# Two places a head for the later layers' stages, with square roots, weight roundings and norms on GpSimd, in a one-core decoder layer

## The reference, cut to what matters

```python
x = layernorm(x + attn(x, Wq, Wk, Wv, Wo))          # 32 query heads, 8 key heads of 64, rope, causal
x = layernorm(x + xattn(x, fside, ctx))             # per batch: quantised gate/up product, silu, quantised down product
x = layernorm(x + ffn(x, up, down, scales))         # signs of the weights, relu, 512 -> 2048 -> 512

def quant_linear(x, w):                             # used twice in xattn
    s = max(sqrt(max(colmax|x|, EPS) / max(colmax|w|, EPS)), EPS)
    xs, ws = x / s, w * s
    x_scale, w_scale = rowmax|xs| / 127, rowmax|ws| / 127
    return (round(xs / x_scale) @ round(ws / w_scale).T) * x_scale * w_scale.T

def layernorm(x): return (x - mean(x)) / sqrt(var(x) + 1e-5)
```

## Time and profile before

| | us |
|---|---|
| median of three executions | 1481.77 |
| lowest and highest | 1480.76, 1482.88 |
| profiled execution, its own time | 1484.37 |
| its span, first to last instruction | 1482.6 |
| PE, DVE, ACT, POOL busy | 1313.8, 998.1, 940.2, 751.6 |

### The profile page before, as it was taken

The page is one execution under the profiler, slowest core; times in us unless marked ns, Lnnn a source line. Parts: engine busy times, 40 slices in busy tenths (PEclk is TensorE's granted clock), DMA queues, the critical chain, the costliest instruction groups (busy, mean ns, idle before and its releaser), DMA issues.

```text
span 1482.6 us, 25047 instructions
## 1 busy us (share of the span) xinstructions
PE 1313.8 (89%) x7099; PEld 1081.3 (73%) x7112; DVE 998.1 (67%) x2435; ACT 940.2 (63%) x2197; POOL 751.6 (51%) x641
## 2 busy tenths in 40 slices
PE   3799999999999999898889888878897889899996
PEld 2588888888888877677777777767776667677775
DVE  3467777767777767878776786778777676744222
ACT  2576677676777776676767766666776584644332
POOL 3456555556556665465535464556441263536343
PEclk9799999999999999999999999999999999999999
DMA  4422212222122233222122222221235311010000
GB/s 170 147 75 65 58 50 67 64 78 60 50 61 58 72 89 100 72 64 58 50 62 76 58 51 58 79 57 47 52 86 162 139 37 49 18 40 3 26 29 28
DMA packets 54852, 98.78 MB, mean 67 GB/s; under 512 B 11744, under 2 KB 13792, under 8 KB 53728
## 3 DMA queue, kind: packets, MB, share of 16 engines
q1 hardware_dynamic: 54752, 97.57, 23.3%
HBM read 51.39 MB, written 4.19 MB: 37 GB/s over the span
## 4 chain that ended last, share of the span: by engine, by line
PE 63%; DVE 14%; ACT 10%; issue 7%; POOL 4%; DMA 1%; ACTq 0%; DVEq 0%; POOLq 0%; SPq 0%
PE m L1588 26%; PE ps_s L1588 8%; PE ps_o L1645 6%; PE ps_t L1633 6%; PE m L1873 6%; PE ps_s L1887 3%; PE ps_t L1887 3%; ACT pT_hi L1028 2%; DVE pT_lo L1308 2%; PE m L1655 2%; ACT probs L1020 2%; DVE o_sum L1261 1%; DVE probs L1247 1%; POOL y L963 1%; DVE sm_a L1361 1%
## 5 line engine op out<-in xcount | busy, mean ns | idle before, releaser
L1020 ACT ACTIVATE probs<-probs,neg_max 128x128 f32<-128x128 f32 (+3 forms) x512 | 285.2, 559 | 179.0 <-DVE neg_max L1247 178.4
L1308 DVE TENSOR_TENSOR pT_lo<-ps_t,pT_hi 128x512 fp32r<-128x512 f32 (+1 forms) x384 | 220.7, 595 | 148.0 <-ACT pT_hi L1028 145.8
L1633 PE MATMUL ps_t<-ident,probs 128*128 128x128 f32 x1280 | 188.3, 278 | 91.8 <-DVE pT_lo L1308 76.3
L1588 PE MATMUL ps_s<-k_st,q_st 128*128 128x256 f32 (+2 forms) x1024 | 236.0, 354 | 0.3 <-DVE neg_max L1247 0.3
L1633 PEld LDWEIGHTS ps_t<-ident,probs 128*128 128x128 f32 x1280 | 146.3, 142 | 122.4 <-DVE pT_lo L1308 94.8
L1247 DVE CUSTOM_DVE_ANT_0 probs<-ps_s,mask 128x128 f32<-128x128 f32 (+3 forms) x512 | 228.1, 482 | 6.8 <-PE ps_s L1588 6.6
L881 POOL TENSOR_TENSOR o_lo<-o_sum,o_hi 128x512 fp32r<-128x512 f32 x64 | 82.7, 1293 | 252.1 <-ACT o_hi L1042 252.1
L1028 ACT ACTIVATE pT_hi<-ps_t 128x512 fp32r<-128x512 f32 (+1 forms) x384 | 185.7, 518 | 5.6 <-PE ps_t L1633 2.5
L934 POOL TENSOR_TENSOR hid_lo<-hid,hid_hi 128x512 fp32r<-128x512 f32 x64 | 83.9, 1313 | 166.2 <-ACT hid_hi L1212 166.1
L1645 PE MATMUL ps_o<-pT_hi,v_st 128*128 128x256 f32 (+2 forms) x512 | 167.8, 339 | 0.0
L1588 PEld LDWEIGHTS ps_s<-k_st,q_st 128*128 128x128 f32 x1024 | 154.0, 195 | 4.0 <-DVE neg_max L1247 0.5
(11 more groups left out here) (251 smaller groups left out, 3064.9 us busy)
## 6 DMA issues: line engine op xcount, KB each, us to landing
q_st<-q_tmp SPq DMA_DIRECT2D x512, 64.0 KB, 2.0
raw<-in_wq_t SPq DMA_DIRECT2D x32, 256.0 KB, 3.0
k_st<-k_st SPq DMA_DIRECT2D x64, 128.0 KB, 2.4
raw<-in_wo_t SPq DMA_DIRECT2D x32, 256.0 KB, 3.0
raw_b<-in_ffn_t SPq DMA_DIRECT2D x10, 512.0 KB, 7.5
y<-in_x_t SPq DMA_DIRECT2D x4, 1024.0 KB, 10.8
raw<-in_wkv_t SPq DMA_DIRECT2D x16, 256.0 KB, 3.7
y<-in_x SPq DMA_DIRECT2D x4, 1024.0 KB, 5.7
```

Of the source, the lines that this page charges most:

```text
L1020: act.activation(probs[:, h % 2, SO[i]:SO[i] + SW[i]], probs[:, h % 2, SO[i]:SO[i] + SW[i]], ACT.Exp, bias=neg_max[:, h % 2, i:i + 1], sca ...
L1308: dve.tensor_tensor(pT_lo[:, d, :], ps_t[:, (h + k) % 2, 0:P * w].rearrange("p (w c) -> p w c", c=P), f32(pT_hi[:, d, :]), ALU.subtract).t ...
L1588: i = pe.matmul(dst, a, c, start=(j == 0), stop=(j == len(terms) - 1))
L1633: i = pe.transpose(ps_t[:, (h + k) % 2, P * c:P * (c + 1)], probs[:, h % 2, at:at + P], ident[:, :])
```

## The change: two places a head, smaller stages, and work moved to GpSimd

- **Places.** Every engine but SP has two places for stages. DVE: `dve` after the first low part and the sum of the old head, `dve2` right after the reciprocal. ACT: `act` after `high_p(2)`, `act2` at the end. PE: `pe` before the third group of transposes, `pe2` right before `values`. POOL's places are at the start of b, after `repeat_r(0)` (ticks with h = 2) and after `rotate_k` (h = 3); SP's at the start of b and before `move_k`.
- **Stages.** Norms, roundings and `add` go one tile a stage; `scales` is a stage of its own (`xscale`, `wscale`). A new hand-placed schedule for ticks 0 to 72; that of the ticks from 64 on is shifted.
- **Work.** All 20 square roots become a `pow` with exponent 0.5 or -0.5 on POOL (128x4 elements; the norms' reciprocals on DVE go). The centring products of N and B move from DVE to POOL, those of F stay. The roundings of all weights, and those of `xs` for batches 0 and 1, move from ACT to POOL.
- **Timing of the batches.** The last third of batch 1's chain A (its row and its four products, silu and `a`) falls into ticks 66 to 72. Batch 1's chain B starts at tick 73, not 67, and its `x2T` at 92, not 88. Batch 2's `wmax` and the load for it come after tick 64. Four of six signs in steps 8 to 15 move past tick 64.

```diff
-A_SLOW = """
-    0 dve colmax0 colmax1
-    1 dve colmax2 colmax3
...
-    7 dve xabs0 xabs1
-    8 act xround0
-    9 act xround1
...
+A_0 = """
...
+    6 dve2 colmax0
+    7 dve colmax1
+    8 dve colmax2
+    9 dve colmax3
+    9 pe2 colx
+    10 dve ratio
+    11 pool root
+    11 dve2 reps
...
+    14 dve xabs0
+    14 pool ws0 ws1 ws2 ws3
+    15 dve xabs1
+    16 dve xscale
...
+    18 pool xround0 xround1 xround2 xround3
+    18 dve2 xq
...
+N_0 = """
+    1 dve var0
+    2 dve var1
+    2 dve2 var2
+    3 dve var3
+    4 dve rstd
+    6 pool power norm0 norm1 norm2 norm3
...
+A_1 = """
...
+    62 act wqT0
+    62 pe2 wT1
+    65 act wqT1
+    66 pe wrow
+    66 act wrow
+    67 pe prod0
+    67 dve prod0
...
+    70 dve prod3
+    71 act silu
+    72 dve a
...
-    17 dve var20 var21
-    18 act std2
-    19 dve y20 y21
+    17 dve var20 var21 var22 var23 rstd2
+    18 pool power y20 y21 y22 y23
...
-    7 dve var
-    8 act std
-    12 dve norm
-    12 sp out
+    7 dve var
+    7 pool power
+    9 dve norm
+    10 sp out
...
+    (SLOTS, "N", 2, N_FAST),
     (SLOTS + 1, "T", 0, T_STAGES),
-    (SLOTS + 5, "A", 2, A_FAST),
-    (SLOTS + 3, "B", 1, B_FAST),
-    (SLOTS + 24, "B", 1, X2T),
+    (SLOTS + 7, "A", 2, A_FAST),
+    (SLOTS + 9, "B", 1, B_FAST),
+    (SLOTS + 28, "B", 1, X2T),
...
+            def rounded(tile, scale):
+                return pool.tensor_scalar(tile, tile, scale, ROUND, ALU.mult, ALU.add)
+
+            def centered(n, mv, inv, t):
+                return pool.tensor_scalar(y[:, n, :], y[:, n, :], mv[:, t, 0:1], inv[:, 1, t:t + 1], ALU.subtract, ALU.mult)
...
+                if name == "root":
+                    after(pool, "A", "dve", b, "ratio")
+                    ends(pool.tensor_tensor(sm_a[:, 3, :], sm_a[:, 3, :], half_pow[:, 0, :], ALU.pow), "A", "pool")
+                    return
...
                         high_p(n, h, 2)
                         if h == 1 and nxt:
                             high_q(u + 1, (0, 1))
+                        if half == 1:
+                            later("act", slot(g, b, h))
...
                         if half == 1:
-                            later("act", slot(g, b, h))
+                            later("act2", slot(g, b, h))
...
-                if name == "root":
-                    after(act, "A", "dve", b, "ratio")
-                    i = act.activation(sm_a[:, 3, :], sm_a[:, 3, :], ACT.Sqrt)
...
                             if k == 0 and (prev or h > 0):
                                 add_o(n - 1, (h - 1) % G, u * 2 + (h - 1) // 2)
+                            if k == 0 and half == 1:
+                                later("dve", slot(g, b, h))
...
                         dve.reciprocal(r_inv[:, :, h // 2, h % 2], row_sum[:, h % 2, :]).then_inc(r_done, 1)
+                        if half == 1:
+                            later("dve2", slot(g, b, h))
...
-                        if half == 1:
-                            later("dve", slot(g, b, h))
...
+                        if half == 1:
+                            later("pe", slot(g, b, h))
                         transpose_probs(n, h, 2)
                         if more:
                             scores(*ahead, 2)
                             scores(*ahead, 3)
-                        if half == 1:
-                            later("pe", slot(g, b, h))
...
+                        if half == 1:
+                            later("pe2", slot(g, b, h))
                         values(n, h, b % 2)
...
-                        after(pe, "B", "dve", b, "y21")
+                        after(pe, "B", "pool", b, "y23")
```

More of the change, by code:

```diff
@@ new lines @@
+"""
+N_1 = """
+    9 dve2 var0
+    10 dve2 var1
+    11 dve var2
+    12 dve var3
+    19 dve rstd
+    20 pool power
+    22 pool norm0 norm1 norm2
+    23 pool norm3
+"""
+B_0 = """
+    23 sp wT
+    25 dve2 wmax
+    27 sp w
+    30 dve2 colmax
+    31 pe colx
+    31 dve ratio
+    31 pool root
+    31 dve2 reps
+    32 pe rows
+    32 act roww
+    32 dve2 xs
+    33 dve xabs
+    33 dve2 xscale
+    34 dve wabs
+    34 act xround0
+    34 pool ws0 ws1
+    34 dve2 wscale
+    35 act xround1
+    35 pool wround0
+    35 dve2 xq
+    36 pe xT
+    36 dve wq
+    36 act xqT
+    36 pool wround1
+    36 pe2 wT
+    37 act2 wqT
+    38 pe wrow
+    38 act wrow
+    38 pe2 prod0
+    39 dve prod0
+    39 pool add0
+    39 pe2 prod1
+    40 dve prod1
+    40 pe2 prod2
+    42 dve prod2
+    42 pool add1
+    42 pe2 prod3
+    43 pool add2
+    44 dve prod3
+    45 dve var20
+    45 dve2 var21 var22
+    46 dve var23
+    46 pool add3
+    46 dve2 rstd2
+    47 pool power y20
+    48 pool y21 y22
+    50 pool y23
+    58 pe x2T0
+    58 act hi0
+    58 dve2 lo0
+    59 pe x2T1
+    59 act hi1
+    59 dve2 lo1
+    60 pe x2T2
+    60 act hi2
+    60 dve2 lo2
+    61 pe x2T3
+    61 act2 hi3
+    62 dve lo3
@@ L154 @@
+"""
+N_FAST = """
+    0 dve var0 var1
+    1 dve var2 var3 rstd
+    2 pool power norm0 norm1 norm2 norm3
 """
@@ L173 @@
     2 dve ratio
[L174 to L205, removed]
+    2 pool root
+    3 dve reps
+    4 pe rowsw rowsx
+    4 act roww
+    5 dve xs0 xs1
+    5 pool ws0
+    6 pool ws1
+    7 pool ws2
+    8 pool ws3
+    6 dve xabs0 xabs1 xscale
+    7 act xround0 xround1
+    8 act xround2 xround3
+    9 dve wabs0 wabs1 wscale xq
+    10 pool wround0 wround1
+    10 pe xT0 xT1
+    11 act xqT0 xqT1
+    11 pool wround2 wround3
+    13 dve wq
+    14 pe wT0 wT1
+    14 act wqT0 wqT1
+    16 pe wrow
+    16 act wrow
+    17 pe prod0
+    17 dve prod0
+    18 pe prod1
+    18 dve prod1
+    19 pe prod2
+    19 dve prod2
+    20 pe prod3
+    20 dve prod3
+    20 act silu
+    22 dve a
 """
@@ L210 @@
     2 dve ratio
[L211 to L222, removed]
+    2 pool root
+    3 dve reps
+    4 pe rows
+    4 act roww
+    4 pool ws0
+    5 pool ws1
+    5 dve xs xabs xscale
+    6 act xround0 xround1
+    7 dve wabs wscale xq
+    8 pool wround0 wround1
+    8 pe xT
+    8 act xqT
     10 dve wq
@@ L594, in run @@
                 later(eng, tick)
+                later(eng + "2", tick)
         def tile_of(p, j):
@@ L643, in ends, with at_tick @@
             i.then_inc(done[chain + e], 1)
-        def at_tick(eng, tick):
-            return [(chain, b, name) for e, chain, b, name in SCHEDULE.get(tick, []) if e == eng]
+        def at_tick(place, tick):
+            return SCHEDULE.get((tick, place), [])
         block = es.enter_context(nc.Block())
@@ new lines, in a @@
+                ends(i, "A", "pool")
+            def b_(b, name):
+                if name == "root":
+                    after(pool, "B", "dve", b, "ratio")
+                    ends(pool.tensor_tensor(sm_b[:, 3, 0:2], sm_b[:, 3, 0:2], half_pow[:, 0, 0:2], ALU.pow), "B", "pool")
+                    return
+                if name == "power":
+                    after(pool, "B", "dve", b, "rstd2")
+                    ends(pool.tensor_tensor(norm[:, 1, :], norm[:, 0, :], half_pow[:, 1, :], ALU.pow), "B", "pool")
+                    return
```

406 lines of the change are left out of this document (201 added, 205 removed).

## The result

The changed kernel takes 1503.81 us (median of 4 runs, 1497.09 to 1506.81) against 1481.37 (4 runs), a ratio of 1.0144, 95% interval 1.0104 to 1.0183. The forecast, 1449 with a range up to 1478, was wrong in sign and range. The profiled execution took 1497.09, the fastest of the four, with a span of 1495.3; beside the profiled execution of before (1484.37) that is 12.7 us more, where 32.9 less were forecast. So 45.6 us have to be found.

What follows compares the result with a forecast made beforehand. PE was taken as the bound, with only its waits and clock to win. Seven steps -47.3, last step -3, feed-forward periods +4.4, +5 and +8 gave -32.9 us on 1484.37: 1451.5, as a median 1449, range 1424 to 1478.

Steps and rivals of the forecast that it cites:

- the term for POOL's blocks: Feed-forward periods: five norm and y2 blocks on POOL, 6.1 us each, cost +8 us net, from 0 to 20.
- +4.4: Feed-forward periods: PE gets batch 1's products and row, 4.4 us more.
- +5: Feed-forward periods: batch 1's last low part bare at tick 96, about 2 us, and x2T0 late; together 5 us more.
- PE's own work (15.7): Seven steps: PE's work for later layers, 17.2 us less two transpose groups slipping into the last step, 15.7 kept.
- the 444.9: Seven steps: their time without later layers, seven times the 63.56 us of eight heads of attention alone.
- 18 us left of 64: Seven steps: of 43 us of plain waits and 21 us lost to PE's clock, 18 us remain.
- Rival 3: DVE's first place: stalls only move, staying at some 50 us; 1481 us; chance 0.06.
- ticks 11 and 31: Steps: DVE's reps waits for the power behind rotate_k on POOL, 1.2 + 1.0 us, twice, within the 18.
- the stall at 610 us: Kernel before: two centring products hold DVE 3.99 us; PE's third transposes wait 4.08 us, clock down until about 623.
- Last step: Last step: loses batch 1's products, a table load and four signs, gains 24 transposes, three copies and wq: -3 us.
- 1 (dear power): POOL's queue: 17 places pay each us of a power over the first; at 5 us, 1517 us; chance 0.12.
- 2 (blocks take more: POOL's five blocks and dense queue cost 20 us, not 8, second half keeps 22: 1465 us; chance 0.17.

Runs made afterwards that it cites:

- e8: The changed kernel with twelve more GpSimd instructions of 128x512 behind its end, two of each form: subtract with a pointer 1.56 us, multiply and add with two pointers 0.77.
- e1: The changed kernel with the centring products from tick 64 on back on DVE, powers left on POOL: 1474.4 us, ratio 0.9953.
- e2: The changed kernel with all centring products of the later layers back on DVE, powers left on POOL: 1468.1 us, ratio 0.9919.
- e9: The changed kernel with centring still on POOL in its places, but as multiplication by 1/std and addition of -mean/std: 1468.7 us, ratio 0.9919.
- e12: As e9, with batch 1's down-weight maximum and batch 0's last low part at tick 62 moved to DVE's second place: 1467.5 us, ratio 0.9903.
- e3: The changed kernel with each of its 20 powers done twice, first into unused columns: 1516.5 us, ratio 1.0229.
- e15: As e9, with batch 1's last steps, chain B and x2T earlier, e12's edit, and xq ahead of the weights' maxima in the tail: 1456.8 us, ratio 0.9841.
- e4: The changed kernel with batch 3's whole chain A three ticks later: 1505.0 us, ratio 1.0162.
- e6: As e2, with batch 2's chains A and B two ticks later and batch 3's chain N ten ticks later: 1470.4 us, ratio 0.9922.
- e7: As e2, with only the four column maxima of batch 3's chain A two ticks later: 1468.0 us, ratio 0.9911.

## Why the prediction was wrong

**The step that failed is the price of POOL's centring.** The prediction said: "For a rounding or centring of 128x512 the ends are the one-input copy, 0.65, and the two-input subtraction, 1.28. I take 1.28, as both do arithmetic per element." For the rounding that held from above (0.70 to 0.79). The centring takes 2.07 to 2.14 (e8: the subtraction alone 1.56), and one row for two operations with different arithmetic was not a bound. The five blocks of the tail take 9.3 and not 6.1 us, 16 us more of POOL's time, but e1 puts the cost at 29 us and e2 and e9 the whole of it at 35: a late block is paid again by what stands behind it and by PE's clock (0.86 in the first period). In the sum it sits in the term for POOL's blocks, +8, from 0 to 20. With all other terms of the tail as forecast (334.3 us) that term came out at 32.5, far above its upper end, and the range of the whole was too narrow with it.

**How much that explains.** By the medians the forecast is 54.8 us too low (1503.8 against 1449), and 35 to 36 of them go with the centring on POOL or its dear form (e2, e9). The kernel without them, at 1468, is inside the range but still 19 us over the forecast: that rest is mostly the steps, below.

**The tail, once that is taken out, is near the forecast, in part by luck:** 341.2 us in e2 against 342.3. But the forecast had 25.6 us of centring on POOL in it, and e2 has none there; e9, whose blocks stay on POOL and take 4.5 us where I had 6.1, has 346.7. So something else in the tail costs more than I gave it, and the single terms (+4.4, +5) were not measured. The two places that I named are there, `x2T0` late behind the y2 block (8.73 us) and the last low part bare at tick 96 (5.16, I had about 2 for it). What I did not see is the longest: the norm block of batch 3 ahead of `ws3`. I counted what waits for `hid_lo` behind the block and not what else stands behind it in the same queue.

**The steps: 478.6 forecast, 498.6 measured, 492.0 without the centring on POOL.** This is the second term that failed. With PE's own work (15.7) and the 444.9 taken as they were, the "18 us left of 64", a judgement, should have been 31 (492.0 - 444.9 - 15.7), with the centring on POOL 38; PEclk came to 0.98, not the 0.99 that I asked for. The part that I named went: the wait for the low part is 14.9 us, under the 25 that I set. In its place came the wait of the reciprocals' transposes, 23.1 from 5.4. Rival 3 ("The first place lies between two low parts, so it delays the very instruction PE waits for") was right in its mechanism for part of the time: in e12 two stages moved from the first place to the second cut the last step by 3.3 us or more. In ticks 11 and 31 I gave DVE's wait for the power 2.2 us each; it was 1.44 and 0.54. I missed tick 48, where the power stands behind two centred tiles: 4.73.

**What the prediction misread in the rows.** It blames the stall at 610 us on the size of the stage: "two centring products keep DVE for 3.99 us in one place". In the trace of before these are one product of 3.54 us and one of 0.53, and the long one ends 0.3 us after a row of four two-input instructions on POOL. The last section shows the same in the changed kernel. So the size of the stage alone does not explain that stall.

**Last step:** -3 forecast, +0.85 measured, two waits of 3.3 and 4.5 us for DVE's first place; e12 brings it to 57.6, the forecast being 58.4.

**What was right.** The power at 1.0 us. The Trainium skill (GPSIMD Engine Reference, 2.1 Instruction dispatch) has the first call of a freshly loaded routine pay some 6 us that show as no instruction. This trace does not show it: the first block in the steps, POOL in order of time,

```profile
611.94 0.60 POOL L964 COPY r_rep<-r_inv 128x512 f32<-128x512 f32 x1
612.51 1.02 POOL L1091 TENSOR_TENSOR norm_n<-norm_n,half_pow 128x4 f32<-128x4 f32 x1
613.63 8.26 POOL L1037 TENSOR_SCALAR y<-y,mv_n,norm_n 128x512 f32<-128x512 f32 x4
```

has no gap ahead of the first power or the first centring, and is as long as the later ones (8.24 and 8.25), so nothing of the 45.6 us is owed to it. Also the table loads: 21 in the whole run before, 4 after, silu's two among them. And the cover of the roundings: four take 2.70 us at 717.82, and POOL then still waits 4.85 us for `o_hi`.

**The rivals.** 1 (dear power) is refuted by the power's own rows, 1.0 us, and by e3. 2 (blocks take more, 1465, chance 0.17) had the place and too small a price. None had both: slower through the centring. I gave "slower" to the operation that looked exotic, and no doubt to the one that looked like its neighbours.

## What to carry to other kernels

A row of another operation with the same shape doesn't bound an operation's price: on GpSimd, `tensor_scalar` with a subtraction of a pointer scalar cost 1.56 us where a multiplication and addition cost 0.77, so (y - mean)/std was better written y/std + (-mean/std). It isn't the subtraction as such: as `tensor_tensor` a subtraction (`hid_lo`, 1.29) and a multiplication (`w_gu`, 1.26) cost alike. Only the form itself, measured, tells. When a block is put in an in-order queue, list everything behind it until its consumer is due, not only the stage that you fear for; here a norm that wasn't needed for sixteen ticks held one weight tile and through it DVE and PE. And before a whole schedule is rewritten, try its cheapest part alone: eight square roots moved in the steps gave 15 us, no less than the whole new schedule with its centring made cheap (e9, 12; the two intervals overlap), and only e15 is clearly past it.

## What the runs showed that I had not expected

- GpSimd's `tensor_scalar` on 128x512 float32: multiply and add 0.62 us with two immediates, 0.69 with one pointer, 0.77 with two; subtract 1.56, subtract and multiply 2.00 to 2.08 (e8). A power on 128x4 takes 1.0 us and on 128x2 0.71, so a part of it goes by the element.
- On DVE the same centring of 128x512 took 0.84 us (the last norms, 16 of them), and 0.60 and 0.70 in the two groups of e2:

```profile
L1678 DVE TENSOR_SCALAR y<-y,mv_f,norm_f 128x512 f32<-128x512 f32 x16 | 12.4, 835 | 13.0 <-POOL norm_f L1100 13.0
```

- Three edits worth 1.2 to 1.6 us each alone were worth 11.8 together (e15), and three that moved whole chains or one large stage were worth nothing (e4, e6, e7).
- An instruction on DVE can last as long as a row of instructions on POOL. In the changed kernel `xscale` of tick 53, a `tensor_scalar` on 128x4 whose like took as little as 0.14 us, took 4.01, in DVE's first place:

```profile
1033.62 4.01 DVE L1483 TENSOR_SCALAR sm_a<-sm_a 128x4 f32<-128x4 f32 x1
```

POOL in order of time, instructions with two inputs back to back, done at 1037.60:

```profile
1032.60 1.29 POOL L946 TENSOR_TENSOR q_tmp<-q_tmp 128x512 f32<-128x512 f32 x1
1033.85 1.28 POOL L947 TENSOR_TENSOR q_tmp<-q_tmp 128x512 f32<-128x512 f32 x1
1035.09 2.51 POOL L952 TENSOR_TENSOR q_tmp<-q_tmp 128x512 fp32r<-128x512 f32 x2
```

DVE's instruction ends at 1037.63, and PE then has waited 2.14 us for the low part behind it. The kernel before has the like at 984.36 (3.19 us, until 987.55; POOL until 987.53). It doesn't explain the slower tail: what DVE's `tensor_scalar`s take over the shortest of their form sums to 15.6 us in the tail of before and to 15.1 after, in the steps to 14.8 and 9.7. No run takes POOL's row away, so the link is one of times and not tested.
